# Attention and an FP4 feed-forward on one core: first row tiles turned on TensorE, a second output bank in the last batch, a new written order

## The reference

```
xn  = layernorm(x)
qkv = xn @ w_qkv                              # 512 -> 1536
windows of 4 rows every 2 rows, 8 heads of 64:
    attn = softmax(q k^T * 512**-0.5);  o = attn v
    y = o @ w_out + b_out, added into the rows of its window
ffn: linear(x, w) = fp4(x) @ fp4(w)^T         # fp4: blocks of 16, scale = max|x|/6
    h = silu(linear(xn, w_gate)) * linear(xn, w_up)    # 512 -> 1408
    f = linear(h, w_down)                              # 1408 -> 512
out = x + attention(xn) + f
```

## Time and profile before

| | |
|---|---|
| median of three runs | 2207.1 us (2204.01 to 2210.74) |
| the profiled execution: its time | 2204.8 us |
| its span, first to last instruction | 2202.7 us |
| TensorE's granted clock, mean | 1.00 |
| busy share | PE 98%, DVE 76%, POOL 55%, ACT 30% |
| until TensorE's first product | 33.1 us |
| attention up to the feed-forward's first matmul | 829.2 us |

### The profile page before, as it was taken

The page is one execution under the profiler, slowest core; times in us unless marked ns, Lnnn a source line. Parts: engine busy times, 40 slices in busy tenths (PEclk is TensorE's granted clock), DMA queues, the critical chain, the costliest instruction groups (busy, mean ns, idle before and its releaser), DMA issues.

```text
span 2202.7 us, 46918 instructions
## 1 busy us (share of the span) xinstructions
PE 2148.9 (98%) x16712; PEld 1037.8 (47%) x16712; DVE 1663.7 (76%) x3108; ACT 656.9 (30%) x1009; POOL 1219.0 (55%) x877
## 2 busy tenths in 40 slices
PE   4999999999999989999999999999999999999999
PEld 1544444544444444444444444444444444444444
DVE  7877877787787666877878778787787777878774
ACT  2342433333343322222222222222222232222221
POOL 3256767666665554555555555555555555555553
PEclk9999999999999999999999999999999999999999
DMA  9656656575766544333333333433334333343333
GB/s 267 189 122 175 157 142 175 133 191 133 177 149 167 136 166 111 82 87 83 78 90 80 87 83 78 94 75 87 86 80 91 77 83 89 77 92 74 87 74 68
DMA packets 449418, 251.82 MB, mean 114 GB/s; under 512 B 367282, under 2 KB 373938, under 8 KB 449300
## 3 DMA queue, kind: packets, MB, share of 16 engines
q1 hardware_dynamic: 448404, 246.99, 46.1%
q10 hardware_dynamic: 576, 2.10, 0.2%
q0 software_dynamic: 320, 0.97, 0.2%
HBM read 99.01 MB, written 59.77 MB: 72 GB/s over the span
## 4 chain that ended last, share of the span: by engine, by line
PE 75%; POOL 10%; issue 9%; DVE 2%; DMA 1%; SPq 0%; ACT 0%; POOLq 0%; DVEq 0%; ACTq 0%
PE acc L978 10%; PE prj L1350 7%; PE ops L1350 7%; PE acc L1331 5%; PE acc L1335 5%; PE acc L1332 5%; PE prj L978 3%; PE ops L1352 3%; PE prj L1352 3%; PE sps L1333 2%; PE acc L1334 2%; PE sps L1336 2%; PE acc L1336 2%; PE sps L1334 2%; PE acc L1333 2%
## 5 line engine op out<-in xcount | busy, mean ns | idle before, releaser
L978 PE MATMUL acc<-late 128*128 128x512 f16 x2304 | 516.8, 380 | 11.0 <-DMA late<-xh 10.9
L978 PEld LDWEIGHTS acc<-late 128*128 128x128 f16 x2304 | 218.4, 98 | 270.7 <-issue 16.5
L209 POOL TENSOR_TENSOR qk<-qk,xh 128x1408 f32<-128x1408 f32 x64 | 165.6, 2588 | 230.1 <-DVE qk L246 230.1
L1225 DVE SCALAR_TENSOR_TENSOR qk<-acc,row_gains,xh 128x512 f32<-128x512 f32 x64 | 48.0, 751 | 260.2 <-ACT xh L1290 260.2
L204 POOL TENSOR_TENSOR qk<-qk,xh 128x1024 f32<-128x1024 f32 (+1 forms) x128 | 177.3, 1386 | 111.2 <-DVE xh L225 111.2
L214 POOL TENSOR_TENSOR v<-qk,v 128x1408 f16<-128x1408 f32 x64 | 183.0, 2859 | 100.3 <-ACT v L256 100.3
L1350 PE MATMUL prj<-late,qk 128*128 128x512 f16 x704 | 214.6, 379 | 0.7 <-DMA qk<-v 0.7
L1350 PE MATMUL ops<-late,qk 128*128 128x512 f16 x704 | 214.6, 379 | 0.0
L256 ACT ACTIVATE v<-qk 128x1408 f16<-128x1408 f32 x64 | 88.1, 1377 | 367.3 <-POOL qk L209 367.3
L1331 PE MATMUL acc<-late,turned 128*128 128x512 f16 x512 | 194.0, 379 | 0.4 <-DVE qk L1225 0.4
L1335 PE MATMUL acc<-late,turned 128*128 128x512 f16 x512 | 194.1, 379 | 0.0
(11 more groups left out here) (158 smaller groups left out, 4440.0 us busy)
## 6 DMA issues: line engine op xcount, KB each, us to landing
normed<-late SPq DMA_DIRECT2D x64, 256.0 KB, 3.0
res<-in_L_attn_x SPq DMA_DIRECT2D x64, 256.0 KB, 2.9
attended<-res SPq DMA_DIRECT2D x64, 256.0 KB, 2.5
raw<-normed SPq DMA_DIRECT2D x64, 256.0 KB, 2.7
v<-attended SPq DMA_DIRECT2D x64, 256.0 KB, 2.7
out<-v SPq DMA_DIRECT2D x64, 256.0 KB, 2.0
late<-in_L_attn_x SPq DMA_DIRECT2D x62, 256.0 KB, 3.8
ready<-turned SPq DMA_DIRECT2D x36, 256.0 KB
```

Source lines behind the costliest of these rows:

```text
L209: pool.tensor_tensor(blocks(v), blocks(v), spread(s[3]), ALU.mult).then_inc(q["valued"], 1)
L978: last = pe.matmul(out, lhsT, rhs, start=(at == 0), stop=(at == n - 1))
```

## The change

The edit has three parts.

**First rows on TensorE.** In batch 0, tiles 0 to 3 are no longer turned by DMA. TensorE transposes each in eight pieces of 128 by 128 (`turn_first_rows`, `T0` to `T3`) against the identity `eye`, into a bank that is free then (`flip`, the two `sps` and two `ops` banks read as float16), and ScalarE copies the bank to `xt` (`rows_turned`, `y0` to `y3`) and signals what the DMA did.

**Two banks for the last output products.** In the last batch, outside the loop, `p_i` with odd i goes to `acc[2]` and with even i to `prj`, and waits for `final` of i-2 in place of i-1. The feed-forward's second product, which uses `acc[2]`, waits for the last `final` too.

**A new order** on all engines, all four strings. Two waits of the weight transposes for step 0 now name the whole batch before. Each attend step remains a single step.

The core of the diff (of the order strings only TensorE's head is shown):

```diff
+    flip = [bank.bitcast(F16).rearrange("p (a k t) -> p a k t", a=2, k=KC)
+            for bank in (sps[:, 0, :], sps[:, 1, :], ops[:, 0, :], ops[:, 1, :])]
+    flipped = sem("flipped")
+    def out_bank(b, i):
+        return acc[2] if isinstance(b, int) and b == B - 1 and i % 2 else prj
...
-            pool.wait_ge(p_turned, at(b, ATT, a - 2))
+            pool.wait_ge(p_turned, at(b, ATT, a - 2 if a else -1))
...
-            dve.scalar_tensor_tensor(res[:, i % 4, :], prj[:, :], sc[:, 5:6], res[:, i % 4, :],
+            dve.scalar_tensor_tensor(res[:, i % 4, :], out_bank(b, i)[:, :], sc[:, 5:6], res[:, i % 4, :],
...
+        def rows_turned(b, i):
+            act.wait_ge(flipped, i + 1)
+            act.activation(xt[:, :, :, i * P:(i + 1) * P], flip[i], ACT.Copy).then_inc(xt_in[i], 16)
...
+        def turn_first_rows(b, i):
+            pe.wait_ge(c_in, 32)
+            pe.wait_ge(xlo_done, at(b, TPB, i))
+            for a in range(2):
+                for k in range(KC):
+                    last = pe.transpose(flip[i][:, a, k, :], xh[:, i, a, k * P:(k + 1) * P], eye[:, :])
+            last.then_inc(flipped, 1)
...
             pe.wait_ge(o_lo, at(b, TPB, i))
-            pe.wait_ge(final, at(b, TPB, i - 1))
-            three_products(prj[:, :], ...
+            if isinstance(b, int) and b == B - 1:
+                pe.wait_ge(final, at(b, TPB, max(i - 2, -1)))
+                if i == 1:
+                    pe.wait_ge(qkv_out, at(b, QKV, QKV - 1))
+            else:
+                pe.wait_ge(final, at(b, TPB, i - 1))
+            three_products(out_bank(b, i)[:, :], ...
...
-                "M0 q0 q1 q2 q3 q4 q5 q6 q7 v0 s0 v1 s1 v2 M1 s2 v3 q8 q9 q10 q11 q12 q13 q14 s3 q15 v4 s5 v5 s4 a0 "
+                "T0 T1 T2 T3 M0 q0 q1 q2 q3 q4 q5 q6 q7 v0 s0 s1 M1 v1 v2 s2 v3 q8 q9 q10 q11 q12 q13 q14 q15 v4 v5 "
...
-    acc_free = [ended.copied, ended.copied + ended.masked, ended.masked + ended.evacuated]
+    acc_free = [ended.copied, ended.copied + ended.masked + ended.projected, ended.masked + ended.evacuated]
```

More of the change, by code:

```diff
@@ L754, in turn_weights @@
             dve.wait_ge(p_spread, at(b, ATT, a))
-            dve.wait_ge(pv_done, at(b, ATT, a - 2))
+            dve.wait_ge(pv_done, at(b, ATT, a - 2 if a else -1))
             dve.transpose(pt[:, a % 2].rearrange("p h q -> p (h q)"),
@@ L947, in first_rounder @@
         def first_rounder(b, k):
+            if k == 1:
+                act.wait_ge(rows.q["rounded"], 1)
             rounder(act, rows.q, rows.raw[:, k, :], rows.rounder, k)
@@ L955, in scalar @@
         batches(act,
[8 rows of a table removed]
-                {"x": high_rows, "q": qk_out, "v": v_out, "e": exponential, "o": attended, "h": out_high,
[8 rows of a table added]
+                {"x": high_rows, "y": rows_turned, "q": qk_out, "v": v_out, "e": exponential, "o": attended, "h": out_high,
                  "B": unit_rounder, "H": high_unit, "W": weights_high, "U": out_weights_high,
@@ L1049, in project_out @@
             pe.wait_ge(o_lo, at(b, TPB, i))
-            pe.wait_ge(final, at(b, TPB, i - 1))
-            three_products(prj[:, :], [((oh[:, i % 4, 0, k], oh[:, i % 4, 1, k]),
+            if isinstance(b, int) and b == B - 1:
[4 more added lines that the diff above has]
+                pe.wait_ge(final, at(b, TPB, i - 1))
+            three_products(out_bank(b, i)[:, :], [((oh[:, i % 4, 0, k], oh[:, i % 4, 1, k]),
                                                (wo[:, 0, k], wo[:, 1, k])) for k in range(KC)]).then_inc(proj_done, 1)
@@ L1076, in tensor @@
         batches(pe,
[6 rows of a table removed]
-                {"q": project_qk, "v": project_v, "s": scores, "a": attend, "p": project_out, "M": column_tops, "W": out_ready,
[7 rows of a table added]
+                {"q": project_qk, "v": project_v, "s": scores, "a": attend, "p": project_out, "T": turn_first_rows,
+                 "M": column_tops, "W": out_ready,
                  "F": first_products})
```

## The result

The changed kernel takes 2241.0 us (median of 4 runs, 2237.4 to 2246.3) against 2206.0 (2204.0 to 2210.7) for the kernel before: a ratio of 1.0158, 95% interval 1.0129 to 1.0186. The forecast was 2193, with 2185 to 2204 as its range. The profiled execution of the changed kernel took 2237.4 us, its span is 2235.6.

A forecast was written before the change was run, and what follows sets the result against it. TensorE was taken as the bound, at work 2148.9 of 2202.7 us. Gains of 6.9 (start) + 5 (last batch) + 2 (loop) = 13.9 us from 2204.8 give 2190.9, 2193 on the median's scale; range 2185 to 2204.

The forecast's parts named there:

- The start: Before the first product: its wait for the DMA transposes goes, so it starts at about 26.2 us, 6.9 us earlier.
- the other estimate: First row tiles: by the Trainium skill's times, eight transposes take 2.2 to 3.1 us and the start gains 4 to 5.
- q8: Product needing tiles 4 to 7, still turned by DMA: due at 61.6 us, tiles landed by 59 at most, 2.6 us left.
- The cold start: First products on TensorE run at about half pace; this loss of 1 to 2 us was left as it is.
- The last batch: Output products of the last batch: a second bank removes waits, net 5 us gained, bounds 2 and 7.
- The seven waits: Last batch: TensorE's waits for VectorE to empty the one output-product bank, 5.3 us, all go.
- I take 2 us gained for the loop in all, with 7 us either way: Six loop passes: new order, same work, 2 us gained in all, 7 us either way.
- New waits I can bound only by the slack: Loop, p0 behind a4: stands 5.9 us behind instead of 7.9; its operand was ready 7.1 us behind.
- The third rival: Loop, p0 behind o0: a wait every pass from VectorE's edge sums; 2.8 us a pass, 16.8 in all, 2210 us; chance 0.08.
- fewer turns between big and small products: Loop: 11 turns a pass instead of 14, each costing about 0.1 us, 1.8 us gained.
- 0.80 on faster: Whole kernel: chance 0.80 that the measured time is below 2200.5 us.
- The range: Whole kernel: gain from 3 us (start 5, last batch 2, loop 4 lost) to 22 (9, 6, 7), 2185 to 2204.

The follow-up runs named there:

- before_jump: The kernel before, with only TensorE's backward jump moved ahead of its last two products, so nothing is queued behind it: 2231.6 us, ratio 1.0119.
- before_bank: The kernel before with only the second bank for odd output products of the last batch: 2205.6 us, ratio 1.0008.
- before_light: The kernel before with a lighter rounding on VectorE (32 of 512 columns, weights not rounded as they should be): 2199.3 us, ratio 0.9962.
- after_jump: The changed kernel with TensorE's loop body ending behind four products, the attend step a3 opening the next pass: 2226.5 us, ratio 1.0095.
- after_jump_waits: after_jump with w7 exchanged with m0 on VectorE, and low half o2 with rounding l7 on GpSimd: 2225.1 us, ratio 1.0085.

## Why the prediction was wrong

**The start: right in mechanism, with some luck in the gain.** `q0` at 25.8 (forecast 26.2), its releaser the low piece, transposes at 1.01 us for eight (taken as 1, and not the 2.2 to 3.1 of the other estimate), tile 3's ready by 21.4. `q8` did not wait. The gain of 7.3 us is against one trace, in which `q0` stood late: `before_jump`, `before_bank` and `before_light` leave the head as it was and have `q0` at 31.2, 30.8 and 30.3 us instead of 33.1, so against them it is 4.5 to 5.4. And nothing was charged for what follows behind `q0`: 3.0 us are lost again before the loop's first cut. The cold start is 0.9 us longer (26.08 for 25.15), a score step waits 1.09, an attend step 1.00.

**The last batch: the waits for the bank right, the gain wrong.** The seven waits, 5.3 us, fell to two, 1.1 us, and the last products follow 2.6 us apart. But four attend steps in a row wait 0.91 us each for their one bank, v3 waits 1.19, and p7' runs in 4.19 us for 2.75, with a granted clock of 0.65. In this stretch TensorE is idle 1.7 us less than before and takes 2.1 us more for the same matmuls. TensorE's timeline there, in the changed kernel:

```profile
829.03 0.69 PE L1069 MATMUL ops<-pt,v 64*64 64x64 f32 x32 [0.91 <-ACT ot L944]
830.64 1.14 PE L1069 MATMUL ops<-pt,ve 64*64 64x64 f32 x32 [0.91 <-ACT ot L944]
832.68 1.13 PE L1069 MATMUL ops<-pt,v 64*64 64x64 f32 x32 [0.91 <-ACT oe L944]
833.75 4.19 PE L995 MATMUL prj<-wo,oh 128*128 128x512 f16 x12
838.87 2.75 PE L995 MATMUL prj<-wo,oh 128*128 128x512 f16 x12 [0.94 <-DVE res L790]
...
856.95 2.75 PE L995 MATMUL prj<-wo,oh 128*128 128x512 f16 x12 [0.19 <-DVE res L790]
859.54 2.75 PE L995 MATMUL acc<-wo,oh 128*128 128x512 f16 x12
```

The second bank does its work in the last two rows. The rows above are the attend steps that the prediction passed over, as it followed the products alone. Net +0.4 for -5: nothing was gained.

**The loop: the step that failed.** "I take 2 us gained for the loop in all, with 7 us either way" measured +36.9. "New waits I can bound only by the slack" was the wrong bound: slack was looked for at `p0` behind `a4` only. The third rival put a slower loop at `p0` behind `o0`; its sign came (passes of 104.8 us, above its 100), but that place is not it (`p0` waits 0.33 us for its low half in `after_jump`). Two things were not looked at. First, what stands at the end of the body: the jump was in the trace of before, 3.6 us long, on the one engine where it hurts, and the new body ends with 0.7 us of work. Covering it gives back 19 us (1.0158 to 1.0070), baring it on the old order costs 26. Second, how little room VectorE has in the new order: `a7` waits 1.9 us for its weights and `p2` 1.1 for its low half in every pass. Less work on VectorE is worth 22 us on the covered new order (1.0070 to 0.9969), of which 8 on the old order too. Which place of VectorE's order makes it late stays open: undoing one of them, with one on GpSimd (`after_jump_waits`), changed nothing, and the place of `w4` was not tried. With both causes gone the new order only equals the old, so the 2 us counted for fewer turns between big and small products do not show either.

**The chances.** 0.80 on faster rested on adding up gains at places the change was aimed at. A new order of all engines has many places at once, and one look at the waits of today says nothing about those that today are just covered. The range took 4 us lost for the loop, where its own "7 us either way" makes 5; either is small beside 36.9.

## What to carry to other kernels

Before a loop's body is reordered, look at the jump of every engine in the trace of before and at how much work is queued on that engine when it begins; keep more than the jump at the end of the body (here two products, 5.2 us, for a jump of 3.7; more did not help, see below). For each step that others wait for, look at what now stands in front of it on its own queue, above all at instructions that themselves wait. Two idle times on the same engine can lie side by side, so test them by taking away both. Before crediting a stage with a gain, cut both traces at the same work, count the instructions in the cut, and compare with more than one trace of the kernel before. And look at what the next stage waits for when it starts earlier.

## What was not expected of the hardware

A taken jump of this loop takes 3.3 to 4.7 us on TensorE, over all runs, and 0.04 to 0.07 on the other engines. It is not the jump as such: in the feed-forward's loop TensorE's takes 0.2 us, in the trace of before:

```profile
L130 PEldq COMPARE_BRANCH  x28: 83/215/248, 940.2 to 2094.8; - x28
```

More work queued in front does not cover more of the long jump. In `after_jump` four products, 10.5 us, stand in front of the jump, and it still begins at 216.8 us, about 3.9 us before their end; in the trace of before it also begins about 3.9 us before the end of `q7`. Two of the jumps of `after_jump` take 4.73 us, and leave `a3` waiting 1.3 to 1.4 us:

```profile
210.24 10.53 PE L995 MATMUL acc<-late 128*128 128x512 f16 x48
...
L120 PEldq COMPARE_BRANCH  x6: 83/3944/4730, 216.8 to 729.3; - x6
...
528.65 0.69 PE L1069 MATMUL ops<-pt,v 64*64 64x64 f32 x32 [1.32 <-issue]
```

The granted clock and the pace mostly agree: it reads 0.50 to 0.65 in the products that took 4.2 to 5.3 us for 2.75. At the first products of the program they do not: the changed kernel runs 10 matmuls in 4.19 us from 25.81, with a granted clock of 1.00.

The queue that brings instructions tells the two loops apart. It moved 12 packets (0.20 MB, 0.8% of the engines' time; the row below) from 224.2 to 322.7 us, one pass of the long body, and 2 packets in the 1200 us from 900 to 2100:

```profile
q8 instruction: 12, 0.20, 0.8%
```

The packets are those of all engines together, but they fit a long body that is fetched anew in each pass and a short one that is not. The Trainium skill, "Runtime: NRT & Kernel Launch", section "Instruction fetch mechanics", says that a taken branch to a target outside the window that is held forces a fetch before execution goes on; the packets fit this, and 3.3 to 4.7 us would be its price here, but that the fetch makes up the jump's time was not tested. It also says that straight code has the fetch mostly hidden; the 4.16 us stop behind 192 small matmuls is a place where it seems not to be, though that the fetch is its cause was not tested. The same skill, "Advanced Engine Details and Errata", section "Control Flow Timing", gives about 108 ns for a compare-and-branch; TensorE's untaken one took 82 to 83 here and the taken ones of the long loop some 35 times the page's figure.
